# A routing gate computed in plain float32 on four column tiles of TensorE, in a graph layer followed by a mixture of experts

## The chip, the cores and the metric

The kernel runs on one core of a Trainium2 chip. The metric is the device time of one execution in microseconds (us), lower is better.

The engines are named as the profile names them: PE is TensorE (matrix products and transposes), PEld its loads of the stationary operand, DVE is VectorE, ACT is ScalarE, POOL is GpSimd, and SP issues most DMAs.

## The reference

Two layers work on `x` of 20000 rows (tokens) by 256 float32. The first is a message-passing layer over 10000 edges, which adds to `x`. The second is a mixture of 8 experts with a hard choice of one expert a token; its gate is what this case is about:

```python
x = x + gnn(layernorm(x), ...)                      # 20000 x 256
h = layernorm(x)                                    # mean and variance of each row
logits = h @ gate_w + gate_b                        # 20000 x 8
probs = softmax(logits); idx = argmax(probs); prb = probs[idx]
pos = position of the token among those of its expert      # kept = pos < 3125
y[token] = (relu(h @ w1[idx] + b1[idx]) @ w2[idx] + b2[idx]) * (prb * kept)
x = x + y
```

## The kernel before, in words

The program has three stages, one after the other, each a block of its own: the edge and node block (up to 363 us of the span), the routing block (363 to about 540 us), and the expert block (from about 540 us to the end). A stage starts when the one before it is done.

The routing block begins with the gate stage, which the change touches. The 20000 tokens lie in 160 tiles of 128 rows; four tiles are a group (`GT` = 4, `GR` = 512 rows, `NG` = 40 groups), and a group's 512 KB are loaded from the output tensor of the first layer into one of `U` = 4 places (line 1028, on SP). A place is loaded again when both readers of its old group are done, `turn` on PE and `statistics` on DVE.

For each group g:

- PE, `turn` (line 1144): 8 transposes of 128 x 128, so that the 256 features lie on the partitions, into one of two PSUM buffers `ps_t`.
- ACT, `turned_rows` (line 1098): copies the turned group into SBUF as `xt_hi`, rounded to the format fp32r.
- DVE, `turned_half` (line 1222): the remainder `xt_lo` = turned rows less `xt_hi`. It frees the PSUM buffer, which `turn` of group g + 2 waits for (`xt_dve`).
- PE, `gate` (lines 1153 and 1157): two products of `xt_hi` with the gate's weights in two parts (16 columns), and two of `xt_lo` with the first part (8 columns), each 512 columns wide, added in PSUM.
- ACT, `by_expert` (line 1104): copies the 16 x 512 sums to `lt`.
- PE, `turn_back` (line 1166): 4 transposes of 16 x 128, so that tokens lie on the partitions again.
- ACT, `take_logits` (line 1108): copies them to `raw_logits`.
- DVE, `statistics` (line 1215): 4 instructions that give mean and variance of each row.
- POOL, once for `CG` = 2 groups (8 tiles): `coefs` (lines 1049 to 1058, seven instructions, the longest a power of -0.5 on line 1057) gives each row's scale, and `scaled_logits` (lines 1069 to 1072, three instructions) adds the two parts, scales, and adds the bias.

The layer norm is thus applied behind the product; the mean is taken out of the gate's weights once, at the start.

The order of the work is written out by hand. PE goes through `turn(g + 1)`, `turn_back(g - 1)`, `gate(g)`; ACT through `turned_rows(g + 1)`, `by_expert(g)`, `take_logits(g - 1)`; DVE through `statistics(g + 1)`, `turned_half(g)`; POOL through `coefs(n)`, `scaled_logits(n - 1)`, behind eight accumulating writes of the first layer that it still has to issue (line 125, to 376 us). Each engine takes its own instructions in this order, and waits on semaphores.

Behind the last group DVE takes the best expert of all tokens (`best`, line 1248), and then counts, sorts and writes the tables of slots; the expert block needs these tables. SP loads the first expert's weights, three loads of 1 MB, right behind the last row load, and ACT rounds them behind `take_logits(39)`.

Of the kernel before, what the change touches and what calls it, by code (L numbers as in the profile page):

```python
# [30 lines left out]
P = 128  # L31
# [830 lines left out]
def routing_block(nc, io, x1, shared, writes, idx_row, put_row, first_block, first_wide, weights, constants):  # L862
# [6 lines left out]
    CG = 2  # L869
    NCO = NG // CG  # L870
    RANKS = 1 << 15
    CC = CG * GT
    with ExitStack() as ctx:
# [25 lines left out]
        centred = sb("centred", [P, 2, NEXP])  # L899
        gate_parts = sb("r_gate_parts", [P, 2, 2, NEXP], F32R)  # L900
        raw_logits = sb("raw_logits", [P, NT, 2 * NEXP])
# [54 lines left out]
        with ExitStack() as of_load:  # L956
            def load_sb(name, shape, dt=F32):
                return of_load.enter_context(nc.sbuf_tensor(name, shape, dt))

            xt_hi = [load_sb(f"xt_hi{h}", [P, 2, GR], F32R) for h in range(2)]  # L960
            xt_lo = [load_sb(f"xt_lo{h}", [P, 2, GR], F32R) for h in range(2)]
            lt = [load_sb(f"lt{h}", [2 * NEXP, GR]) for h in range(2)]
# [7 lines left out]
        ps_l = [banks[:, 4 + h] for h in range(2)]  # L970
        ps_lt = [banks[:2 * NEXP, 6 + h] for h in range(2)]
# [26 lines left out]
        xt_act = sem("xt_act")  # L998
        xt_dve = sem("xt_dve")
# [42 lines left out]
        def _(pool):  # L1042
# [23 lines left out]
            def scaled_logits(n):  # L1066
                t = slice(CC * n, CC * (n + 1))
                pool.wait_ge(logits_taken, CG * (n + 1))
                chain.link(tt(logits[:, t], raw_logits[:, t, :NEXP], raw_logits[:, t, NEXP:], ALU.add))
                chain.link(tt(below[:, t], logits[:, t], stat[:, t, 0].unsqueeze(2).broadcast_to([P, CC, NEXP]),  # L1070
                              ALU.mult))
                tt(logits[:, t], below[:, t], gate_b[:].unsqueeze(1).broadcast_to([P, CC, NEXP]),
                   ALU.add).then_inc(scaled_ready, 1)
# [19 lines left out]
        def _(act):  # L1093
            def turned_rows(g):
                act.wait_ge(turned, g + 1)
                if g >= 2:
                    act.wait_ge(lt_ready, g - 1)
                nc.scalar.copy(xt_hi[g % 2][:], ps_t[g % 2]).then_inc(xt_act, 1)
# [7 lines left out]
            def take_logits(g):  # L1106
                act.wait_ge(logits_ready, g + 1)
                nc.scalar.copy(raw_logits[:, GT * g:GT * (g + 1)],
                               ps_l[g % 2][:, :2 * GT * NEXP].rearrange("p (t e) -> p t e", t=GT)
                               ).then_inc(logits_taken, 1)  # L1110
# [26 lines left out]
        def _(pe):  # L1137
            def turn(g):
                pe.wait_ge(rows_in[g % U], 16 * (g // U + 1))
                if g >= 2:  # L1140
                    pe.wait_ge(xt_dve, g - 1)
                for c in range(2):
                    for t in range(GT):
                        ins = nc.tensor.transpose(ps_t[g % 2][:, c, t * P:(t + 1) * P],
                                                  rows[:, g % U, t, c * P:(c + 1) * P], ident[:])
                ins.then_inc(turned, 1)

            def gate(g):
                pe.wait_ge(xt_act, g + 1)
                if g >= 2:  # L1150
                    pe.wait_ge(lt_taken, g - 1)
                for c in range(2):
                    nc.tensor.matmul(ps_lt[g % 2], gate_parts[:, c].rearrange("p h e -> p (h e)"),
                                     xt_hi[g % 2][:, c], start=c == 0, stop=False)
                pe.wait_ge(xt_dve, g + 1)
                for c in range(2):
                    ins = nc.tensor.matmul(ps_lt[g % 2][:NEXP], gate_parts[:, c, 0], xt_lo[g % 2][:, c],
                                           start=False, stop=c == 1)
                ins.then_inc(lt_ready, 1)

            def turn_back(g):
# [3 lines left out]
                for t in range(GT):  # L1165
                    ins = nc.tensor.transpose(ps_l[g % 2][:, 2 * NEXP * t:2 * NEXP * (t + 1)],
                                              lt[g % 2][:, t * P:(t + 1) * P], ident[:2 * NEXP, :2 * NEXP])
                ins.then_inc(logits_ready, 1)
# [38 lines left out]
        def _(v):  # L1207
# [10 lines left out]
            def turned_half(g):  # L1218
                v.wait_ge(xt_act, g + 1)
                if g >= 2:  # L1220
                    v.wait_ge(lt_ready, g - 1)
                tt(xt_lo[g % 2][:], ps_t[g % 2], xt_hi[g % 2][:].bitcast(F32), ALU.subtract).then_inc(xt_dve, 1)

            nc.vector.memset(mean_of[:], 1 / D).then_inc(mean_ready, 1)
            nc.vector.tensor_copy(before[:], before_f[:])
# [5 lines left out]
            chain.link(tt(centred[:], gate_w[:], ps_mean[:, :NEXP].unsqueeze(1).broadcast_to([P, 2, NEXP]),  # L1231
                          ALU.subtract))
            chain.link(nc.vector.tensor_copy(gate_parts[:, :, 0], centred[:]))
            tt(gate_parts[:, :, 1], centred[:], gate_parts[:, :, 0].bitcast(F32), ALU.subtract).then_inc(gate_ready, 1)
            statistics(0)
            for g in range(NG):
                if g + 1 < NG:
                    statistics(g + 1)
                turned_half(g)
# [595 lines left out]
```

## Time and profile before

| | us |
|---|---|
| median of 3 runs | 1440.65 |
| lowest and highest | 1434.61, 1442.69 |
| the profiled execution: span from its first to its last instruction | 1438.1 |
| gate stage in it: first row load issued, start of `best` | 364.47, 472.54 |
| PE, DVE, ACT, POOL busy in the span | 1225.2, 1006.2, 957.1, 1022.2 |

No time of its own is given for the profiled execution beside its span, which is 2.6 us under the median of the runs.

The profile comes from one execution. A row of the timeline merges like instructions that follow one another ("x8"); its duration runs from the first start to the last end, and for PE the ends overlap the next starts, since matmuls are pipelined. A mean in ns is that of one instruction. In brackets stands how long the engine had been idle, and what released it. A float32 product is recorded as two matmuls and two weight loads. PEclk is the granted clock of TensorE as a share of 2.4 GHz.

### The profile page before, as it was taken

Reading aid. Unit: us, or ns where it says so; the run is one execution under the profiler, and the core shown is the slowest. Engines: PE = TensorE matmul, PEld = TensorE weight load, DVE = VectorE, ACT = ScalarE, POOL = GpSimd, SP = SyncE. Lnnn points to the kernel's source line nnn. Section 1 sums busy time; section 2 is a strip of 40 time slices with the busy share of each in tenths; the row PEclk is TensorE's granted clock in tenths of the full one; section 3 lists DMA queues with packets and bytes.
Section 4 is the critical chain, followed back from the end, with each engine's and each line's share of the span. In section 5 each row is a group of like instructions: output and inputs, shape, how many; then the busy total and the mean of one; then the engine's idle time right before and its main releaser. Section 6 shows DMA issues by size and latency. Waiting matters only on the chain.

```text
span 1438.1 us, 26842 instructions
## 1 busy us (share of the span) xinstructions
PE 1225.2 (85%) x7872; PEld 1073.0 (75%) x7872; DVE 1006.2 (70%) x2153; ACT 957.1 (67%) x2128; POOL 1022.2 (71%) x920
## 2 busy tenths in 40 slices
PE   2477768888799245999999999999999999999993
PEld 0244444555555135999999999999999999999993
DVE  7999996987799893756657555755755575556652
ACT  4788896886467353767767666766766776667672
POOL 7788688885787105777768766777776777768785
PEclk9977777999899586999999999999999999999997
DMA  9889986453867003433433322423432342233333
GB/s 327 240 265 284 280 203 163 67 75 45 227 214 261 6 10 96 104 47 48 107 47 80 79 45 45 110 44 52 107 48 44 48 110 48 44 49 56 51 54 40
DMA packets 132130, 153.55 MB, mean 107 GB/s; under 512 B 17410, under 2 KB 118850, under 8 KB 131926
## 3 DMA queue, kind: packets, MB, share of 16 engines
q0 software_dynamic: 51648, 64.60, 27.6%
q1 hardware_dynamic: 58758, 66.60, 14.2%
q10 hardware_dynamic: 21648, 21.49, 4.5%
q8 instruction: 29, 0.48, 0.1%
q14 instruction: 47, 0.39, 0.1%
HBM read 98.83 MB, written 53.81 MB: 106 GB/s over the span
## 4 chain that ended last, share of the span: by engine, by line
PE 55%; issue 3%; POOL 2%; ACT 1%; DMA 1%; DVE 0%; ACTq 0%; POOLq 0%; DVEq 0%
PE f_ps_y L1636 27%; PE f_ps_h L1624 26%; PE f_ps_x L1614 2%; POOL out L1515 1%; POOL xg L1497 1%; POOL sg L1501 0%; DMA sg<-stat_rows,idx_row 0%; ACT h_all L1564 0%; ACT h_hi L1563 0%; ACT y_all L1574 0%; ACT f_xn L1548 0%; DMA out<-clean,put_now 0%; DMA sg<-stat_rows,idx_now 0%; DVE clean L1701 0%; DVE x_lo L1669 0%
## 5 line engine op out<-in xcount | busy, mean ns | idle before, releaser
L1563 ACT ACTIVATE h_hi<-f_ps_h,c_b 128x384 fp32r<-128x384 f32 (+1 forms) x416 | 237.1, 570 | 262.9 <-PE f_ps_h L1624 262.9
L1674 DVE TENSOR_TENSOR h_lo<-h_all,h_hi 128x768 fp32r<-128x768 f32 (+1 forms) x208 | 184.2, 886 | 256.6 <-ACT h_all L1564 256.1
L1636 PE MATMUL f_ps_y<-w_hi,h_hi 128*128 128x256 f32 x1136 | 325.2, 286 | 0.0
L1636 PE MATMUL f_ps_y<-w_lo,h_hi 128*128 128x256 f32 x1136 | 320.1, 282 | 0.0
L1636 PE MATMUL f_ps_y<-w_hi,h_lo 128*128 128x256 f32 x1136 | 320.0, 282 | 0.0
L1515 POOL DMA_INDIRECT out<-clean,put_now x159 | 262.8, 1653 | 57.5 <-issue 49.1
L1497 POOL DMA_INDIRECT xg<-out,idx_now x159 | 192.7, 1212 | 128.5 <-issue 118.3
L1624 PE MATMUL f_ps_h<-x_hi,w_hi 128*128 128x384 f32 (+1 forms) x832 | 271.9, 327 | 8.0 <-issue 3.5
L1624 PE MATMUL f_ps_h<-x_lo,w_hi 128*128 128x384 f32 (+1 forms) x832 | 269.3, 324 | 0.0
L1624 PE MATMUL f_ps_h<-x_hi,w_lo 128*128 128x384 f32 (+1 forms) x832 | 269.0, 323 | 0.0
L1564 ACT ACTIVATE h_all<-f_ps_h,c_b 128x384 f32<-128x384 f32 (+1 forms) x416 | 238.1, 572 | 0.0
L1501 POOL DMA_INDIRECT sg<-stat_rows,idx_now x159 | 190.8, 1200 | 49.1 <-issue 48.2
L1636 PEld LDWEIGHTS f_ps_y<-w_hi,h_hi 128*128 128x128 f32 x1136 | 214.0, 188 | 0.3 <-DVE h_lo L1674 0.3
L1636 PEld LDWEIGHTS f_ps_y<-w_lo,h_hi 128*128 128x128 f32 x1136 | 214.3, 189 | 0.0
L1636 PEld LDWEIGHTS f_ps_y<-w_hi,h_lo 128*128 128x128 f32 x1136 | 214.3, 189 | 0.0
L1624 PEld LDWEIGHTS f_ps_h<-x_hi,w_hi 128*128 128x128 f32 x832 | 157.1, 189 | 12.6 <-issue 7.4
L1624 PEld LDWEIGHTS f_ps_h<-x_lo,w_hi 128*128 128x128 f32 x832 | 157.1, 189 | 0.0
L1624 PEld LDWEIGHTS f_ps_h<-x_hi,w_lo 128*128 128x128 f32 x832 | 157.1, 189 | 0.0
L612 PEld LDWEIGHTS ps_agg<-same,msg 128*128 128x128 f32 x320 | 67.8, 229 | 66.7 <-issue 56.9
L601 PE MATMUL ps_w<-fc,hidden 64*128 64x320 f32 x160 | 68.6, 587 | 56.6 <-DVE tmp_h L760 55.8
L612 PE MATMUL ps_agg<-same,msg 128*128 128x512 f32 (+3 forms) x320 | 113.5, 516 | 1.6 <-ACT late_rows L546 1.6
L125 POOL DMA_INDIRECT out<-rows,upd_row x48 | 86.6, 1804 | 28.8 <-DMA out<-rows,upd_row 15.4
(227 smaller groups left out, 2280.7 us busy)
## 6 DMA issues: line engine op xcount, KB each, us to landing
shared<-out SPq DMA_DIRECT2D x40, 512.0 KB, 4.0
w_raw<-in_w SPq DMA_DIRECT2D x16, 1024.0 KB, 7.2
xin<-in_x SPq DMA_DIRECT2D x24, 512.0 KB, 7.0
out<-xin ACTq DMA_DIRECT2D x24, 512.0 KB, 5.2
shared<-in_x SPq DMA_DIRECT2D x16, 512.0 KB, 5.5
out<-shared ACTq DMA_DIRECT2D x16, 512.0 KB, 5.7
dst_row<-in_dst SPq DMA_DIRECT2D x20, 256.0 KB, 4.7
xg<-out,idx_now POOLq DMA_INDIRECT x159
```

The costliest lines, as they stand in the source:

```text
L125: nc.gpsimd.indirect_dma_start(out, bass.IndirectOffsetOnAxis(self.upd_row[:, GT * g + t:GT * g + t + 1].bitcast(U32), 0), rows[:, t, :], ...
L601: ins = nc.tensor.matmul(ps_w[:, t, :5 * MUL], hidden[:, t * P:(t + 1) * P], fc2[:], start=True, stop=True)
L612: ins = nc.tensor.matmul(ps_agg[:, c, t * P:], msg[g % 2][:, t].rearrange("p u j -> p (u j)")[:, c::2], same[g % 2][t][:], start=t == 0, s ...
L1497: nc.gpsimd.indirect_dma_start(xg[:, i, :], None, out, bass.IndirectOffsetOnAxis(idx[:, i, 0:1].bitcast(U32), 0), bounds_check=ROWS - 1).t ...
L1501: nc.gpsimd.indirect_dma_start(sg[:, i, :], None, io["stat"], bass.IndirectOffsetOnAxis(idx[:, i, 1:2].bitcast(U32), 0), bounds_check=P * ...
L1515: nc.gpsimd.indirect_dma_start(out, bass.IndirectOffsetOnAxis(put_now[:, i:i + 1].bitcast(U32), 0), clean[:, i, :], None, bounds_check=ROW ...
L1563: nc.scalar.activation(h_hi[:, f, :n * P], ps_h[:, f % SLOTS, :n * P], ACT.Relu, bias=b1[:, e, f:f + 1])
L1564: nc.scalar.activation(h_all[f // 2 % 2][:, f % 2, :n * P], ps_h[:, f % SLOTS, :n * P], ACT.Relu, bias=b1[:, e, f:f + 1]).then_inc(h_taken, 1)
L1614: ins = nc.tensor.transpose(ps_x[:, c, i * P:(i + 1) * P], xn[:, i, c * P:(c + 1) * P], ident[:])
L1624: ins = nc.tensor.matmul(ps_h[:, f % SLOTS, :tiles * P], weights[s][:, w], x[:, c, :tiles * P], start=n == 0, stop=n == 5)
L1636: ins = nc.tensor.matmul(ps_y[:, i], x[:, f, i * P:(i + 1) * P], weights[s][:, w], start=i != 1 and f == 0 and n == 0, stop=f == KF - 1 an ...
L1674: tt(h_lo[:, pair, :n * P], h_all[j % 2][:, :, :n * P], h_hi[:, pair, :n * P].bitcast(F32), ALU.subtract).then_inc(h_lo_ready, 1)
```

## The change

The gate is no longer split into rounded parts. ACT copies the turned rows as they are (`xt`), and DVE computes no remainder; the product is taken in float32. The gate's weights, 8 columns, are padded with zeros to 32 (`gate_lane`). Each of the four token tiles of a group has a product of its own, of 128 columns, whose 32 result rows go to partitions 0, 32, 64 or 96 of one PSUM bank: four column tiles of the PE array. So `lt` becomes 128 x 128, and one transpose of 128 x 128 takes the place of the four small ones. `ps_t` is freed by ACT's copy. The two parts need not be added on POOL, and POOL works on 16 tiles at a time (`CG` = 4), 10 times in place of 20.

```diff
-    CG = 2
+    CG = 4
     NCO = NG // CG
+    LANE = 32
...
-        centred = sb("centred", [P, 2, NEXP])
-        gate_parts = sb("r_gate_parts", [P, 2, 2, NEXP], F32R)
-        raw_logits = sb("raw_logits", [P, NT, 2 * NEXP])
+        gate_lane = sb("r_gate_lane", [P, 2, LANE])
+        raw_logits = sb("raw_logits", [P, NT, NEXP])
...
-            xt_hi = [load_sb(f"xt_hi{h}", [P, 2, GR], F32R) for h in range(2)]
-            xt_lo = [load_sb(f"xt_lo{h}", [P, 2, GR], F32R) for h in range(2)]
-            lt = [load_sb(f"lt{h}", [2 * NEXP, GR]) for h in range(2)]
+            xt = [load_sb(f"xt{h}", [P, 2, GR]) for h in range(2)]
+            lt = [load_sb(f"lt{h}", [P, P]) for h in range(2)]
...
-        ps_l = [banks[:, 4 + h] for h in range(2)]
-        ps_lt = [banks[:2 * NEXP, 6 + h] for h in range(2)]
+        ps_l = [banks[:, 4 + h, :P] for h in range(2)]
+        ps_lt = [banks[:, 6 + h, :P] for h in range(2)]
...
             def scaled_logits(n):
                 t = slice(CC * n, CC * (n + 1))
                 pool.wait_ge(logits_taken, CG * (n + 1))
-                chain.link(tt(logits[:, t], raw_logits[:, t, :NEXP], raw_logits[:, t, NEXP:], ALU.add))
-                chain.link(tt(below[:, t], logits[:, t], stat[:, t, 0].unsqueeze(2).broadcast_to([P, CC, NEXP]),
+                chain.link(tt(below[:, t], raw_logits[:, t], stat[:, t, 0].unsqueeze(2).broadcast_to([P, CC, NEXP]),
                               ALU.mult))
...
-                nc.scalar.copy(xt_hi[g % 2][:], ps_t[g % 2]).then_inc(xt_act, 1)
+                nc.scalar.copy(xt[g % 2][:], ps_t[g % 2]).then_inc(xt_ready, 1)
...
             def turn(g):
                 pe.wait_ge(rows_in[g % U], 16 * (g // U + 1))
                 if g >= 2:
-                    pe.wait_ge(xt_dve, g - 1)
+                    pe.wait_ge(xt_ready, g - 1)
...
             def gate(g):
-                pe.wait_ge(xt_act, g + 1)
+                pe.wait_ge(xt_ready, g + 1)
                 if g >= 2:
                     pe.wait_ge(lt_taken, g - 1)
                 for c in range(2):
-                    nc.tensor.matmul(ps_lt[g % 2], gate_parts[:, c].rearrange("p h e -> p (h e)"),
-                                     xt_hi[g % 2][:, c], start=c == 0, stop=False)
-                pe.wait_ge(xt_dve, g + 1)
-                for c in range(2):
-                    ins = nc.tensor.matmul(ps_lt[g % 2][:NEXP], gate_parts[:, c, 0], xt_lo[g % 2][:, c],
-                                           start=False, stop=c == 1)
+                    for t in range(GT):
+                        ins = nc.tensor.matmul(ps_lt[g % 2][LANE * t:LANE * (t + 1)], gate_lane[:, c],
+                                               xt[g % 2][:, c, t * P:(t + 1) * P], start=c == 0, stop=c == 1)
                 ins.then_inc(lt_ready, 1)
...
-                for t in range(GT):
-                    ins = nc.tensor.transpose(ps_l[g % 2][:, 2 * NEXP * t:2 * NEXP * (t + 1)],
-                                              lt[g % 2][:, t * P:(t + 1) * P], ident[:2 * NEXP, :2 * NEXP])
-                ins.then_inc(logits_ready, 1)
+                nc.tensor.transpose(ps_l[g % 2], lt[g % 2][:], ident[:]).then_inc(logits_ready, 1)
...
-            def turned_half(g):
-                v.wait_ge(xt_act, g + 1)
-                if g >= 2:
-                    v.wait_ge(lt_ready, g - 1)
-                tt(xt_lo[g % 2][:], ps_t[g % 2], xt_hi[g % 2][:].bitcast(F32), ALU.subtract).then_inc(xt_dve, 1)
...
+            nc.vector.memset(gate_lane[:], 0.0).then_inc(lanes_cleared, 1)
...
-            chain.link(tt(centred[:], gate_w[:], ps_mean[:, :NEXP].unsqueeze(1).broadcast_to([P, 2, NEXP]),
-                          ALU.subtract))
-            chain.link(nc.vector.tensor_copy(gate_parts[:, :, 0], centred[:]))
-            tt(gate_parts[:, :, 1], centred[:], gate_parts[:, :, 0].bitcast(F32), ALU.subtract).then_inc(gate_ready, 1)
-            statistics(0)
+            v.wait_ge(lanes_cleared, 1)
+            tt(gate_lane[:, :, :NEXP], gate_w[:], ps_mean[:, :NEXP].unsqueeze(1).broadcast_to([P, 2, NEXP]),
+               ALU.subtract).then_inc(gate_ready, 1)
             for g in range(NG):
-                if g + 1 < NG:
-                    statistics(g + 1)
-                turned_half(g)
+                statistics(g)
```


`xt_ready` and `lanes_cleared` are the new semaphores; `xt_act` and `xt_dve` are gone.

PE's order at the start of the gate stage. `ident` turns rows (L1144) or turns logits back (L1166); L1153 and L1157 are the gate's products. Before:

```order
L1172 MATMUL banks<-c_gate_w,mean_of 128x8 x2
L1144 MATMUL banks<-c_ident,shared 128x128 x16
L1153 MATMUL banks<-xt_hi,r_gate_parts 16x512 x2
L1157 MATMUL banks<-xt_lo,r_gate_parts 8x512 x2
L1144 MATMUL banks<-c_ident,shared 128x128 x8
L1166 MATMUL banks<-c_ident,lt 128x16 x4
L1153 MATMUL banks<-xt_hi,r_gate_parts 16x512 x2
L1157 MATMUL banks<-xt_lo,r_gate_parts 8x512 x2
```

The same place in the changed kernel, where L1142, L1152 and L1160 are turn, gate and turn_back:

```order
L1164 MATMUL banks<-c_gate_w,mean_of 128x8 x2
L1142 MATMUL banks<-c_ident,shared 128x128 x16
L1152 MATMUL banks<-xt,r_gate_lane 32x128 x8
L1142 MATMUL banks<-c_ident,shared 128x128 x8
L1160 MATMUL banks<-c_ident,lt 128x128
L1152 MATMUL banks<-xt,r_gate_lane 32x128 x8
```

The order of the three parts stays; the gate has eight short products where four long ones stood, and turning back takes one instruction.

POOL's order, one batch of coefficients and logits, before:

```order
L1049 TENSOR_TENSOR half_gap<-stats 128x8
L1050 TENSOR_TENSOR spread<-stats 128x8
L1052 TENSOR_TENSOR square<-half_gap 128x8
L1054 TENSOR_SCALAR spread<-spread 128x8
L1056 TENSOR_TENSOR spread<-spread,square 128x8
L1057 TENSOR_TENSOR inverse<-spread,power 128x8
L1058 TENSOR_SCALAR stat<-inverse 128x8
L1069 TENSOR_TENSOR logits<-raw_logits 128x64
L1070 TENSOR_TENSOR below<-logits,stat 128x64
L1072 TENSOR_TENSOR logits<-below,c_gate_b 128x64
```

And in the changed kernel:

```order
L1048 TENSOR_TENSOR half_gap<-stats 128x16
L1049 TENSOR_TENSOR spread<-stats 128x16
L1051 TENSOR_TENSOR square<-half_gap 128x16
L1053 TENSOR_SCALAR spread<-spread 128x16
L1055 TENSOR_TENSOR spread<-spread,square 128x16
L1056 TENSOR_TENSOR inverse<-spread,power 128x16
L1057 TENSOR_SCALAR stat<-inverse 128x16
L1068 TENSOR_TENSOR below<-raw_logits,stat 128x128
L1070 TENSOR_TENSOR logits<-below,c_gate_b 128x128
```

A batch has one instruction fewer, each of them works on twice the tiles, and the batch comes half as often.

## Rows read from the trace of the kernel before

**Rows 1.** Waits, 396 to 464 us: who waited for whom, us in total, times, longest.

```profile
PEld banks L1157 <- DVE xt_lo L1222: 15.3, 28, 0.6
...
PEld banks L1166 <- ACT lt L1104: 4.7, 28, 0.2
```

**Rows 2.** Timeline, one group: start us, us, engine line op out<-in xcount [idle before].

```profile
406.20 1.41 DVE L1215 BATCH_NORM_STATS2 stats<-shared 128x6 f32<-128x256 f32 x4
...
406.81 1.04 PE L1144 MATMUL banks<-c_ident,shared 128*128 128x128 f32 x8
407.01 0.57 ACT L1104 COPY lt<-banks 16x512 f32<-16x512 f32 x1 [0.54 <-PE banks L1157]
...
407.51 1.22 DVE L1222 TENSOR_TENSOR xt_lo<-banks,xt_hi 128x1024 fp32r<-128x1024 f32 x1
...
407.88 1.01 ACT L1098 CAST xt_hi<-banks 128x1024 fp32r<-128x1024 f32 x1 [0.19 <-PE banks L1144]
...
408.12 0.64 PE L1153 MATMUL banks<-xt_hi,r_gate_parts 128*16 128x512 f32 x2
...
409.25 1.03 PE L1144 MATMUL banks<-c_ident,shared 128*128 128x128 f32 x8
```

**Rows 3.** Timeline of PE alone, a group in which nothing held PE back.

```profile
380.65 1.03 PE L1144 MATMUL banks<-c_ident,shared 128*128 128x128 f32 x8
381.61 0.42 PE L1166 MATMUL banks<-c_ident,lt 16*128 16x16 f32 x4
381.96 0.63 PE L1153 MATMUL banks<-xt_hi,r_gate_parts 128*16 128x512 f32 x2
382.43 0.63 PE L1157 MATMUL banks<-xt_lo,r_gate_parts 128*8 128x512 f32 x2
382.90 0.27 PE L1144 MATMUL banks<-c_ident,shared 128*128 128x128 f32 x1
```

**Rows 4.** Groups by form, 396 to 464 us: busy us, mean ns | idle before.

```profile
L1144 PE MATMUL banks<-c_ident,shared 128*128 128x128 f32 x224 | 29.0, 272 | 0.0
...
L1166 PE MATMUL banks<-c_ident,lt 16*128 16x16 f32 x112 | 11.8, 213 | 0.0
...
L1108 ACT COPY raw_logits<-banks 128x64 f32<-128x64 f32 x28 | 5.5, 197 | 0.0
```

**Rows 5.** Groups by form, PE, 355 to 362 us: float32 products.

```profile
L620 PE MATMUL ps_agg<-lin,agg 128*128 128x128 f32 x16 | 2.1, 281 | 1.2 <-ACT agg L541 1.2
```

**Rows 6.** Groups by form, POOL, whole span.

```profile
L1057 POOL TENSOR_TENSOR inverse<-spread,power 128x8 f32<-128x8 f32 x20 | 33.3, 1666 | 1.6
...
L444 POOL TENSOR_TENSOR node_rstd<-node_var,minus_half 128x16 f32<-128x16 f32 x5 | 14.7, 2938 | 0.4
...
L1069 POOL TENSOR_TENSOR logits<-raw_logits 128x64 f32<-128x64 f32 x20 | 6.4, 318 | 2.5 <-ACT raw_logits L1108 0.9
...
L1062 POOL TENSOR_TENSOR centre<-stats 128x160 f32<-128x160 f32 x1 | 0.7, 682 | 0.0
```

**Rows 7.** Stretches: us, busy us by engine (x), PEclk, DMA share, GB/s.

```profile
20.00:30.00 10.00, 0.00 (x0) 0.00 (x0) 7.89 (x44) 7.58 (x16) 9.01 (x13) 1.00 1.08 355
372.00:376.00 4.00, 4.00 (x15) 2.82 (x16) 4.00 (x10) 1.35 (x2) 3.20 (x3) 0.50 1.15 281
...
384.00:388.00 4.00, 4.00 (x30) 2.73 (x30) 4.00 (x10) 3.09 (x5) 3.55 (x9) 1.00 0.90 295
```

**Rows 8.** The row loads of line 1028: from issue to landing.

```profile
DMA to landing us min/median/max: 3.2/4.0/9.0
```

**Rows 9.** Timeline, the end of the gate stage.

```profile
465.32 1.03 PE L1144 MATMUL banks<-c_ident,shared 128*128 128x128 f32 x8
...
466.18 0.21 POOL L1049 TENSOR_TENSOR half_gap<-stats 128x8 f32<-128x8 f32 x1 [0.51 <-DVE stats L1215]
...
469.44 0.32 POOL L1069 TENSOR_TENSOR logits<-raw_logits 128x64 f32<-128x64 f32 x1
...
472.54 1.49 DVE L1248 TENSOR_REDUCE best<-logits 128x160 f32<-128x1280 f32 x1 [3.89 <-POOL logits L1072]
```

More of the change, by code:

```diff
@@ L997, in routing_block @@
         lt_taken = sem("lt_taken")
-        xt_act = sem("xt_act")
-        xt_dve = sem("xt_dve")
+        xt_ready = sem("xt_ready")
+        lanes_cleared = sem("lanes_cleared")
         logits_ready = sem("logits_ready")
@@ L1108, in take_logits @@
                 nc.scalar.copy(raw_logits[:, GT * g:GT * (g + 1)],
-                               ps_l[g % 2][:, :2 * GT * NEXP].rearrange("p (t e) -> p t e", t=GT)
+                               ps_l[g % 2].rearrange("p (t e) -> p t e", t=GT)[:, :, :NEXP]
                                ).then_inc(logits_taken, 1)
```

## The prediction

> **What bounds the kernel now.** I looked first at where the changed code runs: the gate stage, which ends with the start of `best` on DVE at 472.54 us [rows 9]. The three stages follow one another, and `best` waits for the last logits, so what this stage gains or loses, the program gains or loses whole; the expert block behind it has the same instructions. The question is the period of one group of 512 tokens, times the 34 or so groups that run in a steady state, and what is left at the two ends.
>
> The waits of the steady part come next. PE's load for the products of `xt_lo` waits for DVE's `xt_lo` in each group, 15.3 us over 28 groups (0.55 us each), and for ACT's `lt` 0.17 us each [rows 1]. DVE itself has no wait there: a group costs it 1.41 us of statistics and 1.22 us of remainder, which overlap a little [rows 2]. From one turn to the next it is 409.25 - 406.81 = 2.44 us [rows 2]: DVE sets the period. PE is close behind. Where DVE had not yet caught up, PE ran through a group in 382.90 - 380.65 = 2.25 us without a gap: 0.96 us from turn to turn_back, 0.35 to the products of `xt_hi`, 0.47 to those of `xt_lo`, 0.47 to the next turn [rows 3]. So taking the work off DVE alone would be worth no more than 0.19 us a group; beyond that the new products decide.
>
> As a check: turn of group 39 begins at 465.32 us [rows 9] and that of group 5 at 382.90 us [rows 3]; 82.4 us by 34 is 2.42 us.
>
> **Part by part.** *DVE* loses `turned_half`. What is left is 1.41 us a group [rows 2], and it no longer waits for ACT. It cannot be the bound above that.
>
> *PE, turn*: unchanged, 0.96 us to its successor. Inside, one transpose follows another at (1.04 - 0.272) / 7 = 0.11 us [rows 2, 4], so 0.87 us of it are the eight, and 0.09 us the step to work of another shape.
>
> *PE, turn_back*: four small ones took 0.35 us to the next start [rows 3], (0.42 - 0.213) / 3 = 0.07 us each [rows 3, 4] and 0.07 us for the step. One transpose of 128 columns costs 0.11 us, with the step 0.18 us.
>
> *PE, gate*: eight float32 products of 128 columns. Each is recorded as two matmuls. The nearest row is the first layer's float32 product of 128 columns, 16 records in 2.1 us, (2.1 - 0.281) / 15 = 0.12 us apiece [rows 5]; the transposes of the same width take 0.11 us. With 0.11 us, the 16 records take 1.74 us one after the other. That is the upper end. The lower end is four column tiles wholly side by side: four records deep, 0.44 us. The trace has no two products in different column tiles, so nothing in it says how much they overlap. I take a value between the ends by this reasoning: PE takes its matmuls in the order of the program [rows 2, 3], and the two records of one product go to the same column tile, where the second must wait for the first. The neighbour's first record can then run beside this second record, but no earlier. Eight products then take 8 x 0.11 + 0.11 = 0.98 us. The weight loads, of 32 columns, lie beside the matmuls as all others do in these rows.
>
> With 0.04 us for the step to the next turn (0.47 less two half products' 0.43), PE's period becomes 0.96 + 0.18 + 0.98 + 0.04 = 2.16 us; with the ends of the gate it is 2.92 us or 1.62 us.
>
> The Trainium skill, "TensorE: Matmul & The Clock Gate", section "Part 3: Packing small matmuls", gives 2.38x for three column tiles of 32 columns. No run here shows it. As an estimate from that page, 1.74 / 2.38 = 0.73 us for the gate and a period near 1.9 us, some 19 us off the time; that lies between my value and the lower end.
>
> *ACT*: copying the turned group stays at 1.01 us [rows 2]. `lt` becomes 128 columns in place of 512: a copy of 64 columns took 0.20 us and that of 512 columns 0.57 us [rows 2, 4], so about 0.25 us; `raw_logits` stays near 0.20. Together 1.46 us: under PE's period. Its waits don't bind: the turned group is copied one group ahead of the product that needs it.
>
> *POOL*: the last batch took 469.44 - 466.18 = 3.26 us for the coefficients [rows 9], 1.67 of it the power over 8 columns; over 16 columns a power takes 2.94 us [rows 6]. The other six grow by some 0.03 us each: 4.7 us. The two logits instructions on 128 columns lie between 0.32 us at 64 and 0.68 at 160 columns [rows 6], 0.55 us, and 0.08 to the next: 1.26 us. That is 5.95 us for four groups, 1.49 us a group: hidden. Kept at 8 tiles, it would be 3.26 + 0.1 + 2 x 0.40 us for two groups, about 2.1 us each, and about equal to PE's new period.
>
> *Row loads*: 512 KB in 2.16 us are 243 GB/s; the chip moved 355 GB/s in an earlier stretch [rows 7]. A load lands 4.0 us after its issue [rows 8]; a place comes round every 4 x 2.16 = 8.6 us, of which turn holds it for about 1.2. So the loads stay 3 us ahead. Only at the start are they late: until 384 us the DMA engines are full with the first layer's last writes (share 1.15, and 0.90 after it) [rows 7], so I count no gain before group 5.
>
> *The two ends.* In the first groups PE has half the clock, 0.50 in 372 to 376 us [rows 7]; old and new gate cost about the same there. At the other end `best` began 7.22 us after the last turn [rows 9]. Now: turn 1.03, a wait of 0.19 for ACT, copy 1.01, gate 0.98 and 0.17 for its end, `lt` 0.44 with its wait, turn_back 0.46, `raw_logits` 0.30, POOL 1.26: 5.9 us. POOL's other path, 4.7 + 1.26 + 1.26 = 7.2 us from the last statistics, starts some 2 us before the last turn and ends at 5.2, in time. So the end gives 1.3 us. The weights' first load waits behind the row loads and moves forward with them, and ACT's rounding of it starts earlier by as much, in time for the exponential.
>
> **The sum**: group 39 turns at 382.9 + 34 x 2.16 = 456.3 us in place of 465.3, 9.0 us earlier, and 1.3 us at the end: 10.3 us. The profiled span becomes 1427.8; it lies 2.6 us under the median of the runs, and so the time becomes 1440.65 - 10.3, about **1430 us**. With 0.05 us more or less a group it is 1428.5 to 1432, with 0.1 us 1427 to 1434.
>
> **Rivals.**
>
> *The four tiles run wholly side by side.* The period is 1.62 us, just above ACT, DVE and POOL. 34 x 0.80 = 27.3 us earlier, less about 1.5 us in which the row loads (324 GB/s) are still behind at the start; the end gains nothing, since POOL's path of 7.2 us from the last statistics then ends last. 1440.65 - 25.7: **1415 us**. For it: each product uses 32 of 128 columns, and nothing but the order couples them. Against: the two records of each product. The page's 2.38x would end between this and my forecast, near 1421 us, and is counted here.
>
> *The tiles don't overlap at all.* Period 2.92 us. Group 39 turns at 382.9 + 34 x 2.92 = 482.2 us, 16.9 us later than before; the three groups before group 5 lose 0.5 to 0.7 us each, 2 us, and the end gives 0.5 back: **1459 us**, slower. For it: all float32 rows here run one record after another, and a float32 product costs twice the records. It decides from a gate of more than 2.44 - 0.96 - 0.18 - 0.04 = 1.26 us, that is, when less than about 0.5 us of 1.74 overlaps.
>
> *The gain is eaten by the steps between shapes.* At 0.14 us more at each of the two borders of the gate the period is 2.44 us again, and the time **1440 us**. The rows show steps of 0.04 to 0.09 us between a 128-column transpose and a product of 8 or 16 columns, which speaks against it. The Trainium skill, "TensorEngine Tiling (Array Packing)", section "Key Properties", says that a change of tiling mode drains TensorE; the trace agrees only so far as such a drain costs under 0.1 us, unless the old products were no tiles in its sense.
>
> *TensorE loses its clock.* Now it is granted 1.00 once the stage runs. If it fell to half for half of the new stage, the mean period would be near 3.2 us and the time about 1467 us. PE stays busy nearly throughout in all cases above, so I give it little.
>
> **Chances.** Pairs overlap 0.41, wholly side by side (or near it) 0.27, no overlap 0.16, eaten 0.10, clock 0.06. The likeliest is 1430 us, with a range of its own of 1426 to 1436. The range for all is 1412 to 1453: it holds the first, second and fourth nearly whole and the edge of the third, and leaves out about 0.19. Measurement tells 0.5% (7.2 us) from no change: faster is below 1433.4. That holds four fifths of the first case and all of the second, 0.59; the same, 0.19, the rest of the first and the fourth; slower 0.22.
>
> **What would show it.** In the profile after: turn to turn 2.16 us; the gate's 16 records with starts in pairs, a new pair each 0.11 us; no wait of PE for DVE at all; DVE idle 0.7 us a group, waiting for row loads; `lt` copies of 0.25 us, a power of 2.94 us ten times. 16 starts 0.11 us apart would prove the serial rival, 0.44 us from first to last the parallel one. Wrong would be the whole approach if PE waited for row loads in each group, or for ACT.

## The result, and the profile after

The changed kernel takes 1417.72 us in the median of four runs (1415.53 to 1418.18), the kernel before 1440.51 us (1434.61 to 1442.69). The ratio is 0.9841, with a 95% interval of 0.9817 to 0.9866: 22.8 us, or 1.6%, faster. The forecast was 1430 us. The sign was right and the time lies in the range, but the gain is more than twice the one forecast, so its sum was wrong.

The profiled execution has a span of 1416.1 us. One group of the gate stage in its timeline, from turn_back to the next turn (columns as in [rows 2]; L1142 is turn, L1152 the gate, L1160 turn_back, L1096, L1102 and L1106 the copies on ACT):

```profile
408.06 0.27 PE L1160 MATMUL banks<-c_ident,lt 128*128 128x128 f32 x1
408.26 0.38 PEld L1152 LDWEIGHTS banks<-xt,r_gate_lane 128*32 128x32 f32 x16 [0.17 <-issue]
408.26 1.01 ACT L1096 COPY xt<-banks 128x1024 f32<-128x1024 f32 x1 [0.44 <-PE banks L1142]
408.26 0.64 PE L1152 MATMUL banks<-xt,r_gate_lane 128*32 128x128 f32 x16
...
408.84 1.09 PE L1142 MATMUL banks<-c_ident,shared 128*128 128x128 f32 x8
409.17 0.27 ACT L1102 COPY lt<-banks 128x128 f32<-128x128 f32 x1
409.33 0.20 ACT L1106 COPY raw_logits<-banks 128x32 f32<-128x32 f32 x1
...
409.77 0.27 PE L1160 MATMUL banks<-c_ident,lt 128*128 128x128 f32 x1
...
409.97 0.65 PE L1152 MATMUL banks<-xt,r_gate_lane 128*32 128x128 f32 x16
...
410.55 1.09 PE L1142 MATMUL banks<-c_ident,shared 128*128 128x128 f32 x8
```

This answers to [rows 2]. From turn to turn it is 410.55 - 408.84 = 1.71 us where it was 2.44. The gate's 16 records lie within 0.64 us, each of them 0.28 us long on the mean, so that only 0.37 us pass from the first start to the last; one after another, 15 starts 0.11 us apart would need 1.64 us. In the trace they start in four rounds of four: the starts of one round lie within 0.02 us, and the next round begins 0.11 to 0.13 us later. The forecast had pairs. From its first start to the next turn the gate takes 408.84 - 408.26 = 0.58 us.

The waits of the steady part, here 390 to 435 us, with the columns of [rows 1]:

```profile
DVE stats L1207 <- DMA shared<-out: 9.3, 13, 1.9
POOL half_gap L1048 <- DVE stats L1207: 8.9, 7, 1.9
PEld banks L1152 <- issue: 4.3, 26, 0.2
PEld banks L1142 <- issue: 3.6, 18, 0.2
PEld banks L1142 <- DMA shared<-out: 2.4, 7, 0.8
```

No engine waits for DVE's remainder any more. What PE still waits for is small: 0.17 and 0.20 us of weight loads held back at the two borders of the gate ("issue"), and some row loads. DVE and POOL now wait for the loads. The landing of these loads, as in [rows 8], and two stretches, as in [rows 7]:

```profile
DMA to landing us min/median/max: 3.7/5.5/9.8
```

```profile
363.50:448.70 85.20, 71.75 (x1000) 55.42 (x1000) 56.09 (x162) 54.37 (x127) 63.72 (x99) 0.95 0.95 299
372.00:376.00 4.00, 3.09 (x42) 2.36 (x34) 2.40 (x8) 1.93 (x5) 3.39 (x3) 0.95 1.16 277
```

A load takes 5.5 us to land where it took 4.0, and over the whole stage the DMA share is 0.95 at 299 GB/s. In 372 to 376 us PE is already granted 0.95, that is, nearly throughout the full clock of 2.4 GHz, where it had 0.50 (1.2 GHz) in the kernel before; in the 4 us ahead of it PE was busy for 3.8 us, before for 2.0 us.

Group 5 turns at 380.16 us, group 39 at 441.22 us (the first fence is of PE at the start of the stage, the second is the end of the stage and answers to [rows 9]):

```profile
380.16 1.09 PE L1142 MATMUL banks<-c_ident,shared 128*128 128x128 f32 x8 [0.72 <-DMA shared<-out]
```

```profile
437.81 1.09 PE L1142 MATMUL banks<-c_ident,shared 128*128 128x128 f32 x8 [0.96 <-DMA shared<-out]
...
441.22 1.09 PE L1142 MATMUL banks<-c_ident,shared 128*128 128x128 f32 x8
...
442.23 0.23 POOL L1048 TENSOR_TENSOR half_gap<-stats 128x16 f32<-128x16 f32 x1 [2.52 <-DVE stats L1207]
...
445.24 0.19 ACT L1106 COPY raw_logits<-banks 128x32 f32<-128x32 f32 x1 [0.33 <-PE banks L1160]
...
446.87 0.43 POOL L1068 TENSOR_TENSOR below<-raw_logits,stat 128x128 f32<-128x128 f32 x1
...
448.78 1.49 DVE L1231 TENSOR_REDUCE best<-logits 128x160 f32<-128x1280 f32 x1 [6.63 <-POOL logits L1070]
```

441.22 - 380.16 = 61.06 us by 34 is a mean of 1.80 us: 1.71 us for a group whose rows are there in time, and 0.09 us of waits for row loads. (The expectations below take 1.74 us as this mean, and so count some 2 us too much in 34 periods.) The stage, from the first row load's issue at 363.51 us to `best`, lasts 85.3 us; before, it was 472.54 - 364.47 = 108.1 us. That is 22.8 us, as much as the medians differ. The rest of the program adds up to nearly nothing: the stage began 1.0 us earlier, and what follows `best` lasted 1.8 us longer, 967.3 us against 965.6, with the same instructions.

### The profile page after: what moved, and what is told of

It reads as the page before. It is cut to its first block, busy times and chain, and to the rows that moved or that the text cites. A ratio compares the mean times of both kernels' runs of the same rounds, so it can differ in the third digit from the quotient of the medians.

```text
span 1416.1 us, 27363 instructions
## 1 busy us (share of the span) xinstructions
PE 1199.7 (85%) x8231; PEld 1068.7 (75%) x8232; DVE 963.6 (68%) x2112; ACT 939.9 (66%) x2128; POOL 994.8 (70%) x810
## 4 chain that ended last, share of the span: by engine, by line
PE 53%; issue 4%; POOL 3%; ACT 2%; DMA 1%; DVE 0%; ACTq 0%; POOLq 0%; DVEq 0%
PE f_ps_y L1619 26%; PE f_ps_h L1607 25%; PE f_ps_x L1597 2%; POOL xg L1480 1%; POOL out L1498 1%; POOL sg L1484 1%; ACT h_all L1547 0%; DMA sg<-stat_rows,idx_row 0%; ACT f_xn L1531 0%; ACT h_hi L1546 0%; DMA sg<-stat_rows,idx_now 0%; DMA out<-clean,put_now 0%; ACT y_all L1557 0%; ACT w_hi L1374 0%; DVE clean L1684 0%
## 5 line engine op out<-in xcount | busy, mean ns | idle before, releaser
L612 PE MATMUL ps_agg<-same,msg 128*128 128x512 f32 (+3 forms) x320 | 117.2, 529 | 1.6 <-ACT late_rows L546 1.6
L125 POOL DMA_INDIRECT out<-rows,upd_row x48 | 86.8, 1809 | 26.3 <-issue 14.4
```

The costliest lines, as they stand in the source:

```text
L125: nc.gpsimd.indirect_dma_start(out, bass.IndirectOffsetOnAxis(self.upd_row[:, GT * g + t:GT * g + t + 1].bitcast(U32), 0), rows[:, t, :], ...
L612: ins = nc.tensor.matmul(ps_agg[:, c, t * P:], msg[g % 2][:, t].rearrange("p u j -> p (u j)")[:, c::2], same[g % 2][t][:], start=t == 0, s ...
```

## The experiments

Time is read twice: as the median of the runs, and as the length of the gate stage in the profile, from the issue of its first row load to the start of `best`. The second leaves out the stage before it, which is the same in all of these kernels and yet ended anywhere from 358 to 366 us. Each ratio is to runs of the kernel before that were taken beside the kernel in question (it is not quite the quotient of the two medians). Those runs had medians of 1440.51 us (beside the changed kernel), 1438.89 us (the next four rows), 1436.14 us (the four after them) and 1439.93 us (the last four), so medians of different sets compare only to within some 4 us, and the stage says more.

| kernel | median us | ratio to before (95%) | gate stage us | turn to turn us | mean, groups 5 to 39 |
|---|---|---|---|---|---|
| before | 1440.51 | | 108.1 | 2.44 | 2.42 |
| changed | 1417.72 | 0.9841 (0.9817 to 0.9866) | 85.3 | 1.71 | 1.80 |
| one column tile, 512 columns | 1468.87 | 1.0215 (1.0177 to 1.0252) | 140.4 | 3.21 | 3.22 |
| one column tile, 128 columns | 1472.14 | 1.0233 (1.0198 to 1.0267) | 142.3 | 3.25 | 3.25 |
| tile-major order | 1416.58 | 0.9834 (0.9800 to 0.9868) | 86.8 | 1.73 | 1.85 |
| two column tiles of 64 | 1431.49 | 0.9960 (0.9940 to 0.9980) | 102.8 | 2.27 | 2.27 |
| remainder back on DVE | 1437.87 | 1.0011 (0.9990 to 1.0033) | 107.9 | 2.44 | 2.44 |
| POOL batches of 8 | 1423.62 | 0.9892 (0.9857 to 0.9928) | 94.0 | 1.70 | 1.80 |
| before, POOL batches of 16 | 1439.54 | 1.0017 (1.0000 to 1.0035) | 108.3 | 2.44 | 2.42 |
| 8 weights | 1417.95 | 0.9849 (0.9807 to 0.9891) | 86.3 | 1.69 | 1.81 |
| half the gate | 1328.98 | other routing | 83.5 | 1.49 | 1.73 |
| logits first | 1412.87 | 0.9819 (0.9791 to 0.9847) | 85.6 | 1.71 | 1.80 |
| pairs of groups | 1418.06 | 0.9875 (0.9819 to 0.9932) | 86.9 | 3.19 for two | 1.83 |
| pairs, logits first | 1417.33 | 0.9858 (0.9829 to 0.9887) | 88.2 | 3.13 for two | 1.84 |

**Are the column tiles what makes the product cheap?** First the product in one tile, 512 columns wide:

```diff
-                    for t in range(GT):
-                        ins = nc.tensor.matmul(ps_lt[g % 2][LANE * t:LANE * (t + 1)], gate_lane[:, c],
-                                               xt[g % 2][:, c, t * P:(t + 1) * P], start=c == 0, stop=c == 1)
+                    ins = nc.tensor.matmul(ps_lt[g % 2], gate_lane[:, c], xt[g % 2][:, c], start=c == 0, stop=c == 1)
...
-                nc.tensor.transpose(ps_l[g % 2], lt[g % 2][:], ident[:]).then_inc(logits_ready, 1)
+                for t in range(GT):
+                    ins = nc.tensor.transpose(ps_l[g % 2][:, LANE * t:LANE * (t + 1)],
+                                              lt[g % 2][:, t * P:(t + 1) * P], ident[:LANE, :LANE])
+                ins.then_inc(logits_ready, 1)
```

> The changed kernel with the gate's float32 product in one column tile: two products of 512 columns where eight of 128 stood, and turn_back in four small transposes again. If the gain comes from the column tiles, the gate takes its four records of 512 columns one after another, 4 x 0.43 = 1.71 us and 0.13 us of steps, turn_back 0.35 us, the turn 0.93 us: a period near 3.1 us where the changed kernel has 1.74, 34 x 1.4 = 46 us more, and a time near 1465 us. If a float32 product with 32 weights is cheap by itself, the time stays at 1418 us.

PE's timeline in that run (L1159 is turn_back, L1151 the gate):

```profile
409.16 0.43 PE L1159 MATMUL banks<-c_ident,lt 32*128 32x32 f32 x4
409.52 1.90 PE L1151 MATMUL banks<-xt,r_gate_lane 128*32 128x512 f32 x4
411.35 1.09 PE L1142 MATMUL banks<-c_ident,shared 128*128 128x128 f32 x8
```

The four records take 411.35 - 409.52 = 1.83 us to the next turn, as computed. The stage grew by 55 us, 9 more than expected: 34 periods of 1.42 us more on the mean are 48 of them, the groups before group 5 cost 6 us more, and the end 1 us. Then the eight products of 128 columns, all in one tile (turn_back as in the last diff):

```diff
-                for c in range(2):
-                    for t in range(GT):
...
+                for t in range(GT):
+                    own = slice(t * P, (t + 1) * P)
+                    for c in range(2):
+                        ins = nc.tensor.matmul(ps_lt[g % 2][:, own], gate_lane[:, c], xt[g % 2][:, c, own],
+                                               start=c == 0, stop=c == 1)
```

> As the run with one column tile, but with the gate in eight products of 128 columns, all on partitions 0 to 31. If short products overlap only where they go to different column tiles, 16 records take 16 x 0.11 = 1.74 us, and the time is again near 1465 us. If short products overlap by being short, wherever they go, it stays near 1418 us with turn_back's 0.15 us a group more, 1423 us.

```profile
406.79 0.35 PE L1162 MATMUL banks<-c_ident,lt 32*128 32x32 f32 x3
407.07 1.94 PE L1153 MATMUL banks<-xt,r_gate_lane 128*32 128x128 f32 x16
408.93 1.09 PE L1142 MATMUL banks<-c_ident,shared 128*128 128x128 f32 x8
```

The same 16 records as in the changed kernel, with the same shapes, now last 1.94 us, and 408.93 - 407.07 = 1.86 us pass to the next turn where it is 0.58 us with four column tiles: a factor of 3.2. So the place is what counts: not float32, not 32 weights, not the short products. A float32 product in a single column tile, in place of the one in four, would have made the kernel 2% slower than before.

**Does a waiting record hold back the next one?** This is the step of the forecast that set 0.98 us:

```diff
-                for c in range(2):
-                    for t in range(GT):
+                for t in range(GT):
+                    for c in range(2):
```

> The changed kernel with the eight products of the gate in another order: both feature halves of token tile 0, then both of tile 1, and so on. The theory of the forecast, that PE starts records strictly in the order of the program and a record that must wait for its column tile holds back the ones behind it, gives 4 records one after another in each tile, the last beside the next tile's first: 13 x 0.11 = 1.42 us for the gate, a period near 2.7 us, about 1450 us. If each column tile has a line of its own, and a waiting record doesn't hold the others back, the gate stays at 0.44 us and the time at 1418 us.

```profile
408.56 0.27 PE L1160 MATMUL banks<-c_ident,lt 128*128 128x128 f32 x1
408.77 0.67 PE L1152 MATMUL banks<-xt,r_gate_lane 128*32 128x128 f32 x16
409.36 1.09 PE L1142 MATMUL banks<-c_ident,shared 128*128 128x128 f32 x8
```

Four records for one tile, then four for the next, and still 0.67 us for all (0.60 to the next turn). In the trace the records again start in four rounds of four, 0.11 to 0.13 us from round to round. In one column tile two records never started closer than 0.11 us (the last run), so a round of four must hold one record of each tile: those of tiles 1 to 3 started ahead of tile 0's second record, which stands before them in the program. Nothing held back the neighbours. The time is that of the changed kernel.

**Does the gain grow with the number of tiles?**

```diff
-    LANE = 32
+    LANE = 64
...
-                for c in range(2):
-                    for t in range(GT):
+                for b, c in ((0, 0), (0, 1), (1, 0), (1, 1)):
+                    for t in (2 * b, 2 * b + 1):
...
```

> The changed kernel with two column tiles of 64 in place of four of 32: the gate runs for token tiles 0 and 1, then for 2 and 3; turn_back takes two transposes. If tiles run wholly side by side, the gate is 8 records deep, 0.87 us and 0.13 us of steps, turn_back 0.31 us, the period 0.93 + 0.31 + 1.0 = 2.24 us, 17 us more than the changed kernel: 1435 us. If two records of one product hold back the neighbour, as the forecast had it, it is 8 pairs and one more over two tiles, 9 to 12 records deep, 1.0 to 1.3 us, and 1439 to 1449 us.

```profile
407.77 0.38 PE L1161 MATMUL banks<-c_ident,lt 128*128 128x128 f32 x2
408.09 1.09 PE L1152 MATMUL banks<-xt,r_gate_lane 128*64 128x128 f32 x16
409.11 1.09 PE L1142 MATMUL banks<-c_ident,shared 128*128 128x128 f32 x8
```

From the gate to the next turn 1.02 us, between 0.58 with four tiles and 1.86 with one; the stage is 17.5 us longer than in the changed kernel, 17 were expected, and the ratios differ by 0.0119, which is also 17 us. The theory of full overlap held, that of the forecast (1439 to 1449 us) didn't.

**Was DVE's work the old bound?**

```diff
-                    pe.wait_ge(xt_ready, g - 1)
+                    pe.wait_ge(lanes_cleared, g)
...
+            def turned_half(g):
+                v.wait_ge(xt_ready, g + 1)
+                tt(rest[g % 2][:], ps_t[g % 2], xt[g % 2][:], ALU.subtract).then_inc(lanes_cleared, 1)
...
+            statistics(0)
             for g in range(NG):
-                statistics(g)
+                if g + 1 < NG:
+                    statistics(g + 1)
+                turned_half(g)
```

> The changed kernel with DVE's remainder put back: for each group DVE subtracts the copied from the turned rows (its result is used by nothing), and the PSUM buffer is free only then. The products and the column tiles stay. If DVE's 1.41 + 1.22 us set the old period, it returns to 2.44 us, 34 x 0.70 = 24 us more, about 1440 us, whatever the products cost. If the gain comes from PE's shorter work alone, the time stays at 1418 us.

```profile
408.64 1.06 PE L1143 MATMUL banks<-c_ident,shared 128*128 128x128 f32 x8 [0.69 <-DVE rest L1213]
...
409.74 0.64 PE L1153 MATMUL banks<-xt,r_gate_lane 128*32 128x128 f32 x16
411.08 1.06 PE L1143 MATMUL banks<-c_ident,shared 128*128 128x128 f32 x8 [0.69 <-DVE rest L1213]
```

2.44 us again, with 0.69 us in which PE waits for DVE, and the stage is as long as before. So both halves of the change were needed: with the cheap product alone, nothing is gained.

**POOL's batches**, in the changed kernel (`CG = 2`) and in the kernel before (`CG = 4`):

> The changed kernel with POOL's batches of 8 tiles again. A batch is 3.26 + 0.1 + 2 x 0.40 = 4.16 us, 2.08 us a group, over PE's period of 1.71 us. If POOL then sets the end, it begins at about 376 us and needs 40 x 2.08 = 83 us: the logits are ready near 460 us where they are at 448.8 us, 11 us more, about 1429 us. If POOL is hidden in both, the time is 1417 us, since the last batch is shorter.

```profile
458.57 1.49 DVE L1231 TENSOR_REDUCE best<-logits 128x160 f32<-128x1280 f32 x1 [15.93 <-POOL logits L1070]
```

This is the start of `best` in DVE's timeline.

DVE waits 15.9 us for POOL's logits, and the stage is 8.7 us longer; 11 were expected, the medians say 5.9 and the ratios 7.3. The larger batches are thus worth 6 to 9 us, once PE is faster than POOL.

> The kernel before with nothing but POOL's batches of 16 tiles. Its period of 2.44 us is over POOL's 2.17 us already, so nothing is gained in it, and the last batch is longer: between 1440 and 1442 us. If POOL's batches had held the kernel before back, the time would fall by several us.

```profile
POOL half_gap L1049 <- DVE stats L1215: 14.3, 4, 3.6
```

In the kernel before they only make POOL wait for statistics (the waits in 390 to 435 us); the stage takes 108.3 us in place of 108.1, and the time doesn't move beyond its interval.

**The borders of the gate.**

```diff
+                m = LANE if g < 2 else NEXP
...
-                        ins = nc.tensor.matmul(ps_lt[g % 2][LANE * t:LANE * (t + 1)], gate_lane[:, c],
+                        ins = nc.tensor.matmul(ps_lt[g % 2][LANE * t:LANE * t + m], gate_lane[:, c, :m],
```

> The changed kernel with 8 weights in place of 32 in each product, from the third group on (the other rows of each column tile keep the zeros of the first two). In the changed kernel 0.09 us pass without work at each border of the gate, which the kernel before, with 8 and 16 weights, did not show. If the border comes from weights of 32 columns, the period falls by about 0.2 us to 1.5 us, near DVE's 1.44 us and the row loads, and the time to about 1412 us. If it comes from the column tiles themselves, nothing changes: 1418 us.

```profile
408.62 0.62 PE L1153 MATMUL banks<-xt,r_gate_lane 128*8 128x128 f32 x16
409.17 1.10 PE L1142 MATMUL banks<-c_ident,shared 128*128 128x128 f32 x8
...
410.31 0.62 PE L1153 MATMUL banks<-xt,r_gate_lane 128*8 128x128 f32 x16
```

The turn comes 0.55 us after the gate's first start in place of 0.58, and the period is 1.69 us. The width of the weights hardly matters, and the time is the same.

**What bounds the stage now?** Half of the gate left out (`for c in range(1)`):

> The changed kernel with the gate's product over the first 128 features alone: four products in place of eight. It leaves out half of the sum, so tokens go to other experts and the expert block's length changes; only the gate stage, to the start of best, is compared. If PE sets the period, 0.22 us less make it 1.49 us and the stage 7 us shorter, to about 78 us. If the row loads already set it (299 GB/s on the mean of the stage), the stage stays near 85 us and PE waits for the loads.

```profile
411.79 1.09 PE L1142 MATMUL banks<-c_ident,shared 128*128 128x128 f32 x8
...
412.92 0.43 PE L1152 MATMUL banks<-xt,r_gate_lane 128*32 128x128 f32 x8
413.28 0.98 PE L1142 MATMUL banks<-c_ident,shared 128*128 128x128 f32 x7
```

```profile
PEld banks L1142 <- DMA shared<-out: 9.5, 20, 1.6
...
PE banks L1142 <- DMA shared<-out: 5.0, 8, 1.4
```

The first fence is a group in PE's timeline, the second its waits in 390 to 430 us. Where no load is late the period is 413.28 - 411.79 = 1.49 us, but PE's weight loads wait 9.5 us in 40 for row loads, and the stage is 83.5 us, 1.8 us shorter, where 7 were possible. The row loads are the bound just below PE: the mean period fell only from 1.80 to 1.73 us. What limits the loads is open. In 390 to 430 us they moved 304 GB/s at a DMA share of 0.96, which speaks for the DMA engines; but the same stage moved 361 GB/s in 384 to 388 us of the changed kernel, and for 24.6 of the 40 us here SP waited with the next load until DVE's statistics had freed a place, which speaks for the four places. A run with more places would tell; there is none. Taking two groups at a time, to halve the borders, showed the same:

```diff
+            for k in range(-1, NG // 2 + 1):
+                for step, first in ((turn, 2 * k + 2), (turn_back, 2 * k - 2), (gate, 2 * k)):
+                    for g in (first, first + 1):
...
```

> The changed kernel with two groups taken together: sixteen transposes, two of turn_back, sixteen products, with four buffers of turned rows. The borders of the gate come half as often. PE needs 2 x 0.87 + 0.06 + 0.22 + 0.10 + 0.88 + 0.10 = 3.10 us for two groups, 1.55 us each. If borders cost what the trace shows and the loads keep up (338 GB/s), 40 x 0.15 = 6 us less, 1412 us. If the row loads give out before, 1415 to 1418 us.

```profile
408.23 1.08 PE L1149 MATMUL banks<-xt,r_gate_lane 128*32 128x128 f32 x32
409.24 2.03 PE L1139 MATMUL banks<-c_ident,shared 128*128 128x128 f32 x16
...
412.43 0.77 PE L1139 MATMUL banks<-c_ident,shared 128*128 128x128 f32 x5
```

```profile
PEld banks L1139 <- DMA shared<-out: 5.7, 7, 1.4
PE banks L1139 <- DMA shared<-out: 3.9, 6, 1.2
```

Two groups take 412.43 - 409.24 = 3.19 us where the loads have landed, 1.60 each, and the stage is no shorter: PE's weight loads wait 5.7 us for row loads (the waits in 390 to 430 us), and the mean period is 1.83 us. One of the four runs took 1429.68 us, the others 1415 to 1419.

**The last batch on POOL.**

```diff
             for n in range(NCO):
+                if n == NCO - 1:
+                    scaled_logits(n - 1)
                 coefs(n)
-                if n:
+                if 0 < n < NCO - 1:
                     scaled_logits(n - 1)
```

> The changed kernel with POOL's next-to-last batch of logits ahead of its last batch of coefficients, in the time in which POOL waited for the last statistics. If POOL's path from the last statistics ends last, it is shorter by one batch of logits, 5.6 us in place of 6.5 us, and the time 1417 us, 0.9 us less, too little for the runs to tell. If PE's path ends last, nothing moves in the trace either.

```profile
438.21 0.24 POOL L1048 TENSOR_TENSOR half_gap<-stats 128x16 f32<-128x16 f32 x1 [2.14 <-DVE stats L1209]
...
442.87 0.43 POOL L1068 TENSOR_TENSOR below<-raw_logits,stat 128x128 f32<-128x128 f32 x1
...
443.78 0.69 POOL L1061 TENSOR_TENSOR centre<-stats 128x160 f32<-128x160 f32 x1
```

These are, in POOL's timeline, the first instruction of the last coefficients, the first of the last logits, and what follows them.

From the last statistics to the end of the logits 443.78 - 438.21 = 5.6 us, as computed, against 6.5, and `best` begins 6.8 us after the last turn in place of 7.6. But the runs were 4.8 us faster, which this can't explain: in its profile the gate stage is no shorter (85.6 us), while the first stage, which the edit doesn't touch, ended 5.2 us earlier. Its interval overlaps that of the changed kernel. It may be the best version by 0.9 us; the runs don't show it.

> Both of the last two changes together: 0.9 us less than the run with pairs, between 1411 and 1417 us. If either is without effect, the same as that run.

1417.33 us, and a stage of 88.2 us, longer than with either edit alone. Both edits together brought nothing.

## Why the prediction was wrong

**Right.** The place and the cause: DVE's 2.44 us set the period, and what follows `best` stayed as it was but for 1.8 us. ACT's copies (1.01, 0.27 and 0.20 us), the power of 2.93 us, the turn and the step behind it (0.93 for 0.96 us) and turn_back with its step (0.20 for 0.18 us) came as computed, and POOL's larger batches were needed at the new period.

**The step that failed** is the gate: "the two records of one product go to the same column tile, where the second must wait for the first. The neighbour's first record can then run beside this second record, but no earlier. Eight products then take 8 x 0.11 + 0.11 = 0.98 us." The tiles run wholly side by side, and a record that waits for its tile doesn't hold back another tile's, as the tile-major run shows. From the gate's start to the next turn I had 1.02 us; it is 0.58 us. That is 0.44 of the 0.45 us by which the forecast 2.16 us lie above the 1.71 us of a group without a late load. Within it the border before the next turn went the other way: at 0.44 us for four records deep it took 0.14 us, where I had 0.04 from the rows. A smaller error beside it: I had the row loads 3 us ahead of PE throughout. At the shorter period they are not, and their waits give back 0.09 us a group: the mean is 1.80 us.

The inference was weak because it took the order in which PE starts its records, which the rows show for one tile only, as the rule for four. I had the lower end, 0.44 us, in the text, and the Trainium skill's figure in "TensorE: Matmul & The Clock Gate", section "Part 3: Packing small matmuls", 2.38x for three tiles, pointed that way too. These runs give 3.2x for four tiles and 1.8x for two, borders counted. The page's figure lies between the two, as it should; three tiles were not run here, and for four the measured 3.2 is the number to take.

**The end of the stage** didn't give 1.3 us: `best` begins 448.78 - 441.22 = 7.56 us after the last turn, where it was 7.22. At the shorter period the statistics of the last groups come late with their loads (DVE's last 12 of these instructions, three groups, run in a row from 437.79 to 442.15 us), so they end 0.9 us after the last turn's start, where I had them 2 us before it. POOL's path from there ends last, as the rival of 1415 us had it. It takes 6.5 us where I had 7.2: the coefficients took 4.6 us as computed, but a batch of logits 0.92 us for my 1.26.

**The first groups** gave something where I counted nothing. Group 5 turns 380.16 - 363.51 = 16.65 us after the first row load's issue, where it was 382.90 - 364.47 = 18.43: 1.8 us. Part of it is real: at half the clock (0.50) the new gate took 1.01 us and the old one 1.85, which I had about equal. But part is scatter: the kernel before with batches of 16 needed 17.6 us, and the tile-major order 15.9, the 8 weights 17.3.

**The sum as it was**: from group 5 to group 39 it is 82.42 - 61.06 = 21.4 us, with 1.8 us more in the first groups and 0.3 less at the end: 22.8 us, where I had 9.0, nothing and 1.3. The gate's 0.44 us are 15 us in 34 groups, more than the whole miss of 12.5; the late loads and the end took back part of it. The rival "wholly side by side" had 1415 us, 3 us too low. Its period of 1.62 us is 0.18 too short, half of it borders and half late loads, 6 us in 34 groups; against that, the first groups gained where it had counted a loss.

**The other rivals.** No overlap: its premise was false, and its price near what the two kernels in one tile show, 1469 and 1472 us for 1459; their period is 3.22 and 3.25 us for 2.92, of which 0.17 us are their four small transposes. Steps between shapes: real, about 0.1 us beyond the records' own spacing at each border, but only 0.02 and 0.10 us more than I had counted, not 0.14 at each. The Trainium skill's rule in "TensorEngine Tiling (Array Packing)", section "Key Properties", that a change of tiling mode drains TensorE, fits these 0.17 and 0.20 us of held-back weight loads. In the kernel with all products in one column tile of 32, too, the turn's weight load is held back by 0.20 us. The kernel before had one such border, and I misread it: I took the 0.17 us ahead of turn_back for a wait for ACT's `lt`, as the profile names it, but `lt` had been done for 0.2 us, and in an early group for 0.9 us, where the profile names nothing:

```profile
377.11 0.33 PEld L1166 LDWEIGHTS banks<-c_ident,lt 16*128 16x128 f32 x4 [0.18 <-issue]
```

Its gate, with 8 and 16 weights in fp32r, had no such hold before the turn. What exactly makes the border, and why it is missing there, is open. The clock stayed at 1.00 from 376 to 444 us.

## What to carry to other kernels

A product with few result rows and many columns is worth spreading over the column tiles: the same 16 records went from 1.86 to 0.58 us, and their order didn't matter. It paid only because DVE's remainder went with it. When one engine's relief is to pay, list the periods of all the others, the DMA queue among them, for the new pace: here PE at 2.25 us, POOL at 2.1 and the row loads at about 1.7 all lay within 0.8 us below DVE's 2.44. Where the two ends of an unknown lie a factor of four apart, an argument about the order of records that no row shows shouldn't choose between them.

## What the runs showed of the hardware

- Eight float32 products of 128 columns took 0.58 us to the next turn in four column tiles of 32, 1.02 us in two of 64, and 1.86 us in one. 8 or 32 weights made 0.03 us of difference.
- The order of the products among the column tiles made no difference beyond 0.02 us (0.60 us tile by tile, 0.58 us interleaved): a record that waited for its tile held back no other tile's.
- Row loads of 512 KB held 299 GB/s on the mean of the stage and took 5.5 us to land; at a period of 2.44 us they took 4.0 us, and at 3.2 us 3.5 to 3.6 us.
- The first stage, the same in all kernels, ended anywhere from 358 to 366 us in their profiles, a spread larger than the effect of most of these edits.
